# Moving the buffers of activations by 32 bytes each against the weights in an adaLN and mixture-of-experts kernel

## The reference, cut to what matters

```python
q      = x + braak_embed[stage][..., None]
attn   = softmax(q @ side.T)                      # per sequence, 256 x 256
o      = attn @ side
t      = o * rsqrt(mean(o*o) + 1e-6) * norm_w
w      = top-2 of softmax(t @ gate_w.T), renormalised   # 8 experts
h1_e   = t @ w1.T + 2 * (t @ a1_e.T) @ b1_e.T     # F = 1024, rank 16
h3_e   = t @ w3.T + 2 * (t @ a3_e.T) @ b3_e.T
act_e  = silu(h1_e) * h3_e
out_e  = act_e @ w2.T + 2 * (act_e @ a2_e.T) @ b2_e.T
result = x + sum_e w_e * out_e
```

## Time and profile before

| | us |
|---|---|
| median of three runs | 1313.89 (1313.85 to 1314.8) |
| time of the profiled execution | 1314.02 |
| its span, first to last instruction | 1312.2 |
| busy: TensorE matmuls | 1304.3 (99% of the span) |
| busy: VectorE | 845.3 (64%) |
| busy: ScalarE | 529.0 (40%) |
| busy: GpSimd | 249.8 (19%) |
| granted TensorE clock over the span | 1.00 |

### The profile page before, as it was taken

One profiled execution on the slowest core, in us unless ns is written; L12 is line 12 of the kernel. 1 busy time (PEld: TensorE's weight loads), 2 busy tenths in 40 slices (PEclk: granted clock), 3 DMA queues, 4 the chain that ended last, 5 costly groups with the idle time before them and its releaser, 6 DMA issues.

```text
span 1312.2 us, 18595 instructions
## 1 busy us (share of the span) xinstructions
PE 1304.3 (99%) x7280; PEld 1142.3 (87%) x7280; DVE 845.3 (64%) x1558; ACT 529.0 (40%) x991; POOL 249.8 (19%) x213
## 2 busy tenths in 40 slices
PE   8999999999999999999999999999999999999998
PEld 8999998888888888888888888888888888888887
DVE  6776656756665576656675667556675666565655
ACT  6766653333343344333333334333343343333332
POOL 3556540202011020202020202011020202020200
PEclk9999999999999999999999999999999999999999
DMA  9454810020202020201102020202020101002000
GB/s 294 144 146 150 233 47 32 2 72 1 72 2 73 1 73 1 58 17 32 42 3 72 1 72 2 73 0 73 2 72 1 58 16 43 32 2 71 1 17 16
DMA packets 73583, 69.56 MB, mean 53 GB/s; under 512 B 7050, under 2 KB 64792, under 8 KB 73368
## 3 DMA queue, kind: packets, MB, share of 16 engines
q1 hardware_dynamic: 73184, 68.37, 17.5%
q10 hardware_dynamic: 312, 0.02, 0.0%
HBM read 51.27 MB, written 17.10 MB: 52 GB/s over the span
## 4 chain that ended last, share of the span: by engine, by line
PE 98%; ACT 1%; DVE 1%; DMA 0%; issue 0%; ACTq 0%; DVEq 0%
PE bank L1173 31%; PE bank L1174 31%; PE bank L1175 30%; PE bank L1226 2%; PE bank L1299 2%; PE bank L1277 1%; PE bank L1219 1%; ACT prob L647 0%; ACT qT_hi L630 0%; DMA embed_in<-in_L_cond_braak_embed 0%; ACT kT_hi L631 0%; DVE probT_lo L863 0%; DVE x_out L1117 0%; ACT value_hi L641 0%; PE bank L1193 0%
## 5 line engine op out<-in xcount | busy, mean ns | idle before, releaser
L1048 DVE TENSOR_TENSOR act_a<-silu_a,bank 128x512 f32<-128x512 f32 x128 | 87.8, 686 | 236.0 <-PE bank L1175 219.5
L731 ACT ACTIVATE br_hi<-act_br 128x512 fp32r<-128x512 f32 x128 | 80.9, 632 | 188.3 <-DVE act_br L1059 188.3
L724 ACT ACTIVATE silu_b<-bank 128x512 f32<-128x512 f32 x128 | 76.2, 596 | 187.9 <-PE bank L1175 187.1
L574 POOL TENSOR_TENSOR t_lo<-t_in,t_hi 128x512 fp32r<-128x512 f32 x32 | 40.6, 1290 | 553.2 <-ACT t_hi L711 553.2
L1173 PE MATMUL bank<-w2T_hi,s_hi 128*128 128x256 f32 x512 | 145.1, 283 | 0.0
L1175 PE MATMUL bank<-w2T_hi,s_lo 128*128 128x256 f32 x512 | 144.9, 283 | 0.0
L1174 PE MATMUL bank<-w2T_lo,s_hi 128*128 128x256 f32 x512 | 144.8, 283 | 0.0
L1056 DVE TENSOR_TENSOR act_b<-silu_b,bank 128x512 f32<-128x512 f32 x128 | 88.0, 687 | 81.6 <-PE bank L1175 80.5
L720 ACT ACTIVATE silu_a<-bank 128x512 f32<-128x512 f32 x128 | 76.0, 594 | 157.4 <-PE bank L1175 157.3
L593 POOL TENSOR_TENSOR v_lo<-v_full,v_hi 128x512 fp32r<-128x512 f32 x64 | 94.6, 1510 | 137.3 <-ACT v_hi L716 137.3
L1069 DVE TENSOR_TENSOR br_lo<-act_br,br_hi 128x512 fp32r<-128x512 f32 x128 | 104.8, 819 | 5.3 <-ACT br_hi L731 2.8
(11 more groups left out here) (191 smaller groups left out, 3251.8 us busy)
## 6 DMA issues: line engine op xcount, KB each, us to landing
x_in<-in_x SPq DMA_DIRECT2D x32, 256.0 KB, 3.9
kv<-in_fside_BxSxS SPq DMA_DIRECT2D x32, 256.0 KB, 3.3
t_scratch<-oT SPq DMA_DIRECT2D x32, 256.0 KB, 2.6
t_in<-t_scratch SPq DMA_DIRECT2D x16, 512.0 KB
x_out<-in_x SPq DMA_DIRECT2D x16, 512.0 KB, 3.9
out<-x_out SPq DMA_DIRECT2D x30, 256.0 KB, 3.9
rho<-scale_scratch SPq DMA_DIRECT2D x16, 256.0 KB
rstd<-scale_scratch SPq DMA_DIRECT2D x16, 256.0 KB
```

Source lines behind the costliest of these rows:

```text
L724: nc.scalar.activation(silu_b[:, :], h1_bank[j % 2][:, :], ACT.Silu).then_inc(silu_b_ready, 1)
L731: nc.scalar.activation(br_hi[j % 2][:, :], act_br[j % 2][:, :], ACT.Copy).then_inc(br_hi_ready, 1)
L1048: nc.vector.tensor_tensor(act_a[j % 2][:, :], silu_a[j % 2][:, :], h3_bank[j % 2][:, :], ALU.mult).then_inc(act_a_ready, 1)
```

## The change

A helper `shifted` takes a buffer of 32 bytes before the one asked for. It is used for `t_hi`, `t_lo`, `v_hi`, `v_lo`, `s_hi`, `s_lo`, `br_hi` and `br_lo`, 22 buffers in all. The 32 bytes add up: the first of them (`t_hi0`) begins 32 bytes past a multiple of 512, the second 64, and so on. `t_hi` and `t_lo` begin at 32 to 128, `v_hi` at 160 to 256, `v_lo` at 288 to 384, `s_hi` at 416, 448 and 480, `s_lo` at 0, 32 and 64, `br_hi` at 96 and 128, `br_lo` at 160 and 192, all modulo 512. What lies between them moves along: the masks, `rho`, `rstd` and `v_full` by 128 bytes, the silus and `act` buffers by 384, and `z_a`, `z_b`, `z_hi`, `z_lo`, `y_scaled` and `x_out` by 192. The weights, `t_in` and all buffers of the attention stay where they were. No instruction is added, removed, or put elsewhere.

```diff
+        def shifted(stack, name, shape, dt):
+            sb(stack, name + "_gap", [P, 8])
+            return sb(stack, name, shape, dt)
...
-        t_hi = [sb(late, f"t_hi{k}", [P, DC, TILE], F32R) for k in range(2)]
-        t_lo = [sb(late, f"t_lo{k}", [P, DC, TILE], F32R) for k in range(2)]
+        t_hi = [shifted(late, f"t_hi{k}", [P, DC, TILE], F32R) for k in range(2)]
+        t_lo = [shifted(late, f"t_lo{k}", [P, DC, TILE], F32R) for k in range(2)]
...
-        v_hi = [sb(late, f"v_hi{k}", [ER, TILE], F32R) for k in range(4)]
-        v_lo = [sb(late, f"v_lo{k}", [ER, TILE], F32R) for k in range(4)]
+        v_hi = [shifted(late, f"v_hi{k}", [ER, TILE], F32R) for k in range(4)]
+        v_lo = [shifted(late, f"v_lo{k}", [ER, TILE], F32R) for k in range(4)]
...
-        s_hi = [sb(late, f"s_hi{k}", [P, TILE], F32R) for k in range(S_RING)]
-        s_lo = [sb(late, f"s_lo{k}", [P, TILE], F32R) for k in range(S_RING)]
-        br_hi = [sb(late, f"br_hi{k}", [P, TILE], F32R) for k in range(2)]
-        br_lo = [sb(late, f"br_lo{k}", [P, TILE], F32R) for k in range(2)]
+        s_hi = [shifted(late, f"s_hi{k}", [P, TILE], F32R) for k in range(S_RING)]
+        s_lo = [shifted(late, f"s_lo{k}", [P, TILE], F32R) for k in range(S_RING)]
+        br_hi = [shifted(late, f"br_hi{k}", [P, TILE], F32R) for k in range(2)]
+        br_lo = [shifted(late, f"br_lo{k}", [P, TILE], F32R) for k in range(2)]
```

## The result

| | us |
|---|---|
| after, median of four runs | 1330.86 (1329.93 to 1331.04) |
| before, median of four runs beside them | 1314.35 (1313.85 to 1315.42) |
| ratio | 1.0124, 95% interval 1.0112 to 1.0136 |
| span of the profiled execution, after | 1329.1 |

The change costs 16.5 us. The likeliest case of the prediction, no effect, did not come true; the time lies in the stated range, and within 1 us of the first figure of the slower rival (1330).

What follows compares the result with a forecast made beforehand. TensorE's matmul starts bound the experts' phase. Every term was 0, so 1312.2 us of span plus 1.8 around it gave 1314.0, less 0.1 for the median: 1313.9 us, range 1298 to 1346.

Steps and rivals of the forecast that it cites:

- The likeliest case of the prediction: Whole kernel: the shifted starts have no effect, 1311 to 1317 us; chance 0.49.
- slower rival: TensorE's two streams do better starting at the same place; 8 ns on 2016 matmuls, 1330 us, on all 1346; chance 0.29.
- The bound: Experts' phase: TensorE's number of matmuls times the start-to-start distance sets the time, 226.7 ns for 512 columns, 120 for 256.
- The rival by which VectorE gets slower: VectorE instructions with inputs at different places slow down; 1.56 times its busy time needed, mild form 1319 us; chance 0.04.
- Stationary operands at an odd multiple of 32 cost nothing by themselves: `s` in `down_y`, `z` in `finish_y`: 1728 shifted loads cost 0, since the `hots` load from 96 isn't longer.
- The other engines: Where their accesses lie against TensorE's makes no difference: matmuls take 227 ns alone, 226.7 with VectorE at work.
- The gate: Its slices start in steps of 128 bytes at no cost, though at half rate, with 2.5 ns left over.
- The load beside the matmul: Moving operand and next load sweep through about 512 bytes of distance per 109 ns load, whatever the start; 0 ns for 4032 + 1728.
- the second of the two ways in which the text said the sweep could fail: TensorE's streams lock to each other: the one refused at the first meeting keeps being refused; no size given.
- The 8 ns from the loads of `hots`: Middle of the 3 to 13 ns excess over 226.7 at 512-column matmuls beside which `hots` is loaded from 96.
- The faster rival: TensorE's streams hinder each other at equal starts; 10.8 ns per matmul returns, 1252 us for all, 1298 for a quarter; chance 0.18.
- The tail: Last `x_out` stores, now beginning at 192 modulo 512: taken as 0, at most 0.3 us more.

Runs made afterwards that it cites:

- a32: Against the kernel before: weights, attention's and experts' buffers all begin at 32 modulo 512, unchanged relative to each other; 1314.81 us, ratio 1.0006.
- lo32: Against the kernel before: low halves of the six weights loaded beside 512-column matmuls begin at 32 modulo 512, weights reordered; 1338.26 us, ratio 1.0181.
- s64a2: Against the kernel before: `s`, `br`, `z` and `a2T` begin at 64 modulo 512, the rest stays at 0; 1310.70 us, ratio 0.9971.
- u96: Against the kernel before: one gap of 96 bytes ahead of all experts' buffers, weights at 0 modulo 512; 1335.73 us, ratio 1.0164.
- w192: Against the kernel before: only `w2T` and `b2T` begin 192 bytes past a multiple of 512, weights reordered; 1309.50 us, ratio 0.9964.
- u256: Against the kernel before: one gap of 256 bytes ahead of all experts' buffers, weights at 0 modulo 512; 1314.26 us, ratio 0.9999.

## Why the prediction was right in its range and wrong in its likeliest case

**The bound.** Right. TensorE's starts set the time, in every kernel of this study; no other engine came near the path. The rival by which VectorE gets slower is out: its `act_s` product has a mean of 807 ns after and 806 before.

**Stationary operands at an odd multiple of 32 cost nothing by themselves.** Right as far as it went: `a32` has them all there, and the time of before. The 0 ns for the 1728 matmuls of 256 columns was wrong even so, because shifting `s` and `z` against `w2T` and `b2T` changes the distance: -1.7 ns on each, -2.9 us.

**The other engines.** No run speaks against it. `lo32` moved only operands that TensorE alone reads in this phase, and the steps grew all the same, so the effect needs no other engine. The reading told nothing of TensorE's own two streams, though.

**The gate.** Its row was no witness for this stream. It pays about 2.5 ns over its columns at each of its four starts, at what was read as half the rate, and the matmuls in question pay 13.3 to 20.

**The load beside the matmul.** This is the step that failed. The prediction said that the distance runs once through 512 bytes in each load, whatever it was at the start, and so met the same obstacles before and after; from that it took 0 ns for all 4032. The runs show 4.8 ns on each after, +19.2 us. The 109 ns for a load, from which the sweep was worked out, is the step of the transposes; the load's own record beside a 512-column matmul is 0.19 us long, and no run shows that such a sweep takes place. The 512-column matmuls pay 13.3 ns over their columns at distance 0 and 16 to 20 at the others tried within 256 bytes. The steps after a change of distance aren't constant, and those of `lo32` and `s64a2` depend on what went before. That is the second of the two ways in which the text said the sweep could fail, two streams that lock to each other; that they lock is what the patterns of steps look like, and no run shows the mechanism inside.

The Trainium skill (TensorE: Matmul & The Clock Gate, "Step-by-step: what each phase is for") says that loading the next weights takes no read bandwidth from the running matmul, as the two have independent read ports. The traces don't agree that the running stream is left alone: `lo32` moved only what is loaded, and the step of the matmul beside that load grew by 12 ns.

**The slower rival.** It named the right relation, "the two streams do better when they start at the same place", but split the cost wrongly: 8 ns on the half that begins at odd multiples of 32, 16 us. The runs show 4.8 ns on all 4032 (19.2 us) and -1.7 ns on the 256-column ones (-2.9 us); even and odd multiples are alike (233.3 at 32, 232.7 at 128). The agreement at 1330 is luck in the factors. The 8 ns from the loads of `hots` were near the 6 to 7 ns of most distances, but the rows don't vouch for it: in `u96`, where `br_hi` and `hots` both begin at 96, the seven such steps of the experts' phase still take 230 to 237 ns. So the excess there doesn't come from the distance of that pair alone, and the size is luck as well.

**The faster rival.** Out for the 512-column matmuls: none of the six other distances had a mean under 226.7 ns. It has a true core for the 256-column ones, whose roles are exchanged: they went down to 118 and 113 ns from 120.

**The tail.** The last stores now begin at 192 modulo 512 and land in the same 1.8 us:

```profile
out<-x_out SPq DMA_DIRECT2D x4, 128.0 KB, 1.8
```

From the start of the last matmul to the end of the span it is 3.8 us before and after. The extra beats that the Trainium skill (DMA: Bandwidth & Descriptors, "How a descriptor splits into AXI transactions") names for a start that is no multiple of 256 bytes, up to 0.3 us by the prediction's estimate, can't be seen in either figure.

**What stays open.** Which rule makes a distance good. Distance 160 for the 512-column matmuls was not tried, and no kernel combines 226.7 ns for the one kind with 113 for the other. In `w192` the first phase was 1.7 us longer in the profiled execution (the first matmul with `a13T` at 181.2 us instead of 179.5), which takes back a third of the 5.3 us that the starts gave. Its weights lie in another order, and whether that is the reason wasn't tested. It may be no more than scatter: with the weights in the old order that matmul starts anywhere from 178.7 (`u256`) to 180.9 us (`a32`) in the profiled executions.

## What to carry to other kernels

When matmuls follow each other closely and each loads a new stationary operand, look at the distance from start to start, not at the length of one, and compare it with the columns over the clock. What counted here is where the moving operand begins relative to the one that is loaded beside it, for each kind of matmul apart. Begin with both at equal places, and try a second kind of matmul at an offset of its own. A reason that holds for one meeting of two streams need not hold for a thousand in a row: test it with one uniform shift before arguing on.

## What the runs showed of the hardware

- A common shift of both operands by 32 bytes costs nothing that can be told from no change (1.0006, 0.9997 to 1.0015), and neither does a shift of one by 256 (0.9999, 0.999 to 1.0009). A shift of one against the other by 32, 96, 128, 192 or 224 bytes costs 1.5 to 1.7% of this kernel, 6 to 7 ns on a matmul of 512 columns. With 64 bytes it is 3 ns on those, and the matmuls of 256 columns give the time back (1.0007, 0.9997 to 1.0017).
- The cost reaches beyond the matmul beside the shifted load. In `lo32` the steps are 232.4, 238.6 and 228.6 ns in turn, and only the second has a shifted operand loaded beside it.
- The step between matmuls of 256 columns with a load of 128 columns beside each has at least three steady values: 120 ns with all at one place, and 118 or 113 ns with the moving operand 64 bytes below the loaded one. Both of these occur inside one kernel at the same places, by how the block is entered: in `s64a2` 56 blocks entered by a step of 230 or 231 ns end at 113, and 16 entered by 225 or 226 ns stay at 118.
- The loads' own records hardly show it: 187 to 192 ns in all of these kernels. Only the starts do.
